# Third attention layer: a second staging buffer for the query bands, and the raw keys and value tables loaded at other steps of a head

## The reference, cut to what matters

```
rel = arange(N)[None, :] - arange(N)[:, None]
rp  = clip(rel, -31, 31) + 31                      # 63 buckets
attn = einsum('bhid,bhjd->bhij', q * scale, k)
attn = attn + take_along_axis(einsum('bhid,hdm->bhim', q * scale, rpe_k_table), rp)
attn = attn + swapaxes(take_along_axis(einsum('bhjd,hdm->bhjm', k * scale, rpe_q_table), rp), 2, 3)
attn = softmax(attn)
out  = einsum('bhij,bhjd->bhid', attn, v)
out  = out + (sums of attn over each bucket) @ rpe_v_table
x    = x + layernorm(out @ w_proj.T + b_proj)
```

## Time and profile before

| | |
|---|---|
| median of 3 runs | 2701.12 us (2699.75 to 2709.92) |
| profiled execution, device time | 2711.21 us |
| its span in the trace | 2709.3 us |
| mean granted TensorE clock | 0.83 |
| TensorE matmul / VectorE / ScalarE / GpSimd busy | 72% / 63% / 40% / 31% |
| the layer's loop in the span | from about 1573 to about 2145 us |

### The profile page before, as it was taken

The page is one execution under the profiler, slowest core; times in us unless marked ns, Lnnn a source line. Parts: engine busy times, 40 slices in busy tenths (PEclk is TensorE's granted clock), DMA queues, the critical chain, the costliest instruction groups (busy, mean ns, idle before and its releaser), DMA issues. The chain is left out here.

```text
span 2709.3 us, 46534 instructions
## 1 busy us (share of the span) xinstructions
PE 1963.8 (72%) x16472; PEld 1355.8 (50%) x16472; DVE 1715.2 (63%) x4060; ACT 1091.3 (40%) x2021; POOL 847.5 (31%) x627
## 2 busy tenths in 40 slices
PE   4888884487788873579998367777777729995446
PEld 2555553255555552467777144444444418884334
DVE  3777776575655645679999517767676763225564
ACT  2666662354444431134444215444443303331332
POOL 2000001764444501124443333444444149301001
PEclk8999998799999986679999657877776659997667
DMA  3101111000000000100000565555555240000000
GB/s 97 37 32 36 38 36 57 17 15 15 15 15 15 15 15 4 21 1 21 19 19 10 148 153 129 142 145 149 140 144 132 73 171 17 23 0 8 0 1 18
DMA packets 126467, 145.04 MB, mean 54 GB/s; under 512 B 72472, under 2 KB 100171, under 8 KB 123490
## 3 DMA queue, kind: packets, MB, share of 16 engines
q1 hardware_dynamic: 123040, 132.95, 18.8%
q10 hardware_dynamic: 3266, 9.96, 1.0%
HBM read 94.59 MB, written 40.81 MB: 50 GB/s over the span
## 5 line engine op out<-in xcount | busy, mean ns | idle before, releaser
L407 ACT ACTIVATE l0a_pr<-l0a_sm,l0a_nm 128x512 f32<-128x512 f32 x256 | 185.2, 724 | 147.3 <-DVE l0a_nm L324 146.8
L324 DVE CUSTOM_DVE_ANT_0 l0a_sm<-l0a_ps_s,l0a_tb 128x512 f32<-128x512 f32 x256 | 171.1, 686 | 93.9 <-PE l0a_ps_s L473 90.8
L481 PE MATMUL l0a_ps_p<-top_c_ident,l0a_pr 128*128 128x128 f32 x1024 | 170.4, 290 | 54.1 <-ACT l0a_pT L415 54.1
L2532 DVE STREAM_TRANSPOSE l2a_tt<-l2a_pr 128x1024 f32<-128x1024 f32 x128 | 158.1, 1235 | 73.9 <-ACT l2a_pr L2606 73.9
L2606 ACT ACTIVATE l2a_pr<-l2a_ps_s,l2a_nm 128x512 f32<-128x512 f32 x256 | 174.3, 689 | 67.8 <-DVE l2a_nm L2525 60.4
L2636 PE MATMUL l2a_ps_l<-l2a_tabq,l2a_q 128*128 128x96 f32 x512 | 112.2, 389 | 85.9 <-ACT l2a_staged L2585 80.2
L481 PEld LDWEIGHTS l0a_ps_p<-top_c_ident,l0a_pr 128*128 128x128 f32 x1024 | 110.0, 143 | 117.1 <-ACT l0a_pr L407 64.6
L2525 DVE TENSOR_REDUCE l2a_nm<-l2a_ps_s 128x2 f32<-128x1024 f32 x128 | 156.7, 1224 | 4.4
L2636 PEld LDWEIGHTS l2a_ps_l<-l2a_tabq,l2a_q 128*128 128x128 f32 x512 | 98.3, 286 | 106.0 <-ACT l2a_staged L2585 90.5
L1508 POOL TENSOR_TENSOR l1f_h<-l1f_lm,l1f_sg 128x512 f32<-128x512 f32 x72 | 92.6, 1286 | 183.8 <-DVE l1f_lm L1577 183.8
L2702 PE MATMUL l2a_ps_o<-l2a_tt,l2a_vd 128*32 128x256 f32 (+7 forms) x1472 | 133.6, 394 | 0.0
(11 more groups left out here) (501 smaller groups left out, 5281.1 us busy)
## 6 DMA issues: line engine op xcount, KB each, us to landing
l2a_rawk<-l_k SPq DMA_DIRECT2D x16, 1024.0 KB, 22.8
l2a_qb<-l_qband SPq DMA_DIRECT2D x16, 768.0 KB
l2a_sb<-l_pband SPq DMA_DIRECT2D x32, 384.0 KB
l_qband<-l2a_staged SPq DMA_DIRECT2D x14, 768.0 KB, 19.6
l0a_tb<-l_bias SPq DMA_DIRECT2D x16, 448.0 KB
l2a_ks<-l_k SPq DMA_DIRECT2D x16, 384.0 KB
l_pband<-l2a_pr SPq DMA_DIRECT2D x32, 192.0 KB, 9.0
l_pband<-l2a_pr SPq DMA_DIRECT2D x32, 144.0 KB, 2.9
```

The source lines that it names most:

```text
L324: v.tensor_tensor_reduce(sm[j % 4][:, :], ps_s[j % 2][:, :], tb[slot][:, off:off + N][:, ::-1], -1.0, 3e38, ALU.add, ALU.min, nm[:, j % 4: ...
L407: a.activation(pr[j % 4][:, :], sm[j % 4][:, :], ACT.Exp, bias=nm[:, j % 4:j % 4 + 1], scale=-1.0).then_inc(m["p_ready"], 1)
L481: last = pe.transpose(ps_p[j % 2][:, tile(k)], pr[j % 4][:, tile(k)], ident[:, :])
L2532: v.transpose(tt[n % 2][:, u * NB:(u + 2) * NB, :].rearrange("p (u k) i -> p u (k i)", u=2), pr[g // 2 % PR_RING][:, 2 * (g % 2):2 * (g % ...
```

## The change

`staged` becomes two buffers, used by turns (head modulo 2), and the copy of head h waits for the store of head h-2 and not of h-1. The key bands' rounds move from steps 0 to 2 to steps 1 to 3, on TensorE, on ScalarE and in the numbering. SyncE issues `keys(h + 2)` at step 4 and not 1, and `head_values(h)` at step 5 and not 2. GpSimd makes `values(h + 1)` at step 5 and not 7, and `expand(h + 2)` at step 7 and not 5.

```diff
@@ band_order, and the same in the programs of ScalarE and TensorE
-        if 0 <= h + 1 < HEADS and i < KEY_ROUNDS:
-            order["k", h + 1, i] = len(order) + 1
+        if 0 <= h + 1 < HEADS and 1 <= i <= KEY_ROUNDS:
+            order["k", h + 1, i - 1] = len(order) + 1
@@
-        staged = s.sb("staged", [P, NB, BAND])
+        staged = [s.sb(f"staged{i}", [P, NB, BAND]) for i in range(2)]
@@ SyncE's loop
-                    if i == 1 and h + 2 < HEADS:
-                        keys(h + 2)
                     if i == 3 and 2 <= h + 1 < HEADS:
                         head_scores(h + 1)
-                    if i == 2 and 2 <= h < HEADS:
+                    if i == 4 and h + 2 < HEADS:
+                        keys(h + 2)
+                    if i == 5 and 2 <= h < HEADS:
                         head_values(h)
@@ GpSimd's loop
-                    if i == 5 and h + 2 < HEADS:
+                    if i == 5 and 2 <= h + 1 < HEADS:
+                        values(h + 1)
+                    if i == 7 and h + 2 < HEADS:
                         expand(h + 2)
-                    if i == 7 and 2 <= h + 1 < HEADS:
-                        values(h + 1)
@@ query_evac
-                    if h >= QBAND_RING and r == 0:
-                        before = 0 if h == QBAND_RING else h - 1
+                    if h >= 4 and r == 0:
+                        before = 0 if h == 4 else h - 2
                         a.wait_ge(q_stored[before % QBAND_RING], 16 * (before // QBAND_RING + 1))
```

More of the change, by code:

```diff
@@ L2372, in q_store @@
                     else:
-                        sp.dma_start(qband[h % QBAND_RING][:, 0:ROW], staged[:, :, :].rearrange("p a n -> p (a n)")).then_inc(q_stored[h % QBAND_RING], 16)
+                        sp.dma_start(qband[h % QBAND_RING][:, 0:ROW], staged[h % 2][:, :, :].rearrange("p a n -> p (a n)")).then_inc(q_stored[h % QBAND_RING], 16)
                 def q_load(h):
@@ L2580, in query_evac @@
                     a.wait_ge(m["l_ps"], ROUND["q", h, r])
-                    if h >= QBAND_RING and r == 0:
-                        before = 0 if h == QBAND_RING else h - 1
+                    if h >= 4 and r == 0:
+                        before = 0 if h == 4 else h - 2
                         a.wait_ge(q_stored[before % QBAND_RING], 16 * (before // QBAND_RING + 1))
-                    out = pr[h - 1][:, r, 0:4 * BAND].rearrange("p (a n) -> p a n", n=BAND) if h in (1, 2) else staged[:, 4 * r:4 * r + 4, :]
+                    out = pr[h - 1][:, r, 0:4 * BAND].rearrange("p (a n) -> p a n", n=BAND) if h in (1, 2) else staged[h % 2][:, 4 * r:4 * r + 4, :]
                     a.copy(out, ps_l[:, 0:4 * BAND].rearrange("p (a n) -> p a n", n=BAND)).then_inc(m["l_ready"], 1)
@@ L2616, in _ @@
                     h, i = t // PAIRS, t % PAIRS
-                    if 0 <= h + 1 < HEADS and i < KEY_ROUNDS:
-                        key_evac(h + 1, i)
+                    if 0 <= h + 1 < HEADS and 1 <= i <= KEY_ROUNDS:
+                        key_evac(h + 1, i - 1)
                     if h + 3 < HEADS and i >= 4:
@@ L2734, in _ @@
                         scores(t)
-                    if 0 <= h + 1 < HEADS and i < KEY_ROUNDS:
-                        key_bands(h + 1, i)
+                    if 0 <= h + 1 < HEADS and 1 <= i <= KEY_ROUNDS:
+                        key_bands(h + 1, i - 1)
                     if h + 3 < HEADS and i >= 4:
```

## The result

The kernel after takes 2633.58 us (median of 4 runs, 2631.59 to 2637.26) against 2704.26 us before on the same chip (4 runs): ratio 0.9741, 95% interval 0.9722 to 0.9760, so some 70 us or 2.6% faster. Forecast were 2657 us and 44 us, with a range of 2603 to 2697. The profiled execution has a span of 2630.6 us; that of before has 2709.3, and its device time lay 7 us above the median of its kernel, so the two profiles differ by 8 us more than the medians.

What follows compares the result with a forecast made beforehand. Four DMA engines carrying the skewed loads were taken to bound a head at 31 us, not 34.4. Heads 1 to 12 gain 41 us, head 13 2, head 0 2, less 1: 44 us, so 2657 us, range 2603 to 2697.

Steps and rivals of the forecast that it cites:

- Four engines set the head: Skewed loads with four batches outermost run on four DMA engines, whose queue sets what traffic a head can carry.
- 23 + 7.8 = 31 us a head: Four engines' load: 23 from head 14, 5.2 raw keys, 2.1 store, 0.5 for `kshift` and table; 34.4 us now.
- The 23 us from head 14: Four engines' working time in head 14, which loads no raw keys and stores no query bands: some 23 us.
- Second buffer: ScalarE's wait for `staged`'s store, 9.5 us a head, goes in heads 1 to 12; gain 3.4 us each, 41 in all.
- rival B: The wait only changes its name, as head 13's 33.0 us suggest: gain 17 us or less, 2684 to 2700; chance 0.19.
- Raw keys at step 4: Keys leave the burst at the head's start and land at +28, `xk` ready at +32.8; the move costs nothing.
- a head of at least 29.2 us: Condition of the later keys: `xk` ready at +32.8, wanted by TensorE 3.6 us into the next head.
- Key bands a step later: TensorE and ScalarE work moved from step 0 to 3: taken as 0 us a head; 2 us gained in head 0.
- Compute floor of 25.8 us: Shortest head the compute engines allow, read from heads 14 and 15, which take 25.8 us each.
- Rival A: Keys out of the burst slow nothing, heads fall toward 25.8 us: 2589 us, halfway 2625; range 2589 to 2635, chance 0.23.
- Rival C: Raw keys land later than 33.5 us into a head, TensorE stands in step 1: 65 us slower, 2766 us; chance 0.10.
- SyncE itself is held as well: SyncE's queue in the burst before the change: two issues starting at 1806.21 said to take 5.20 us together.

Runs made afterwards that it cites:

- e4: Kernel after, with each skewed load (query bands, band of the exponentials) issued as four DMAs of one batch each; ratio 0.9465 to the kernel before, median 2558.9 us.
- e5: Kernel before, with both skewed loads split into four DMAs of one batch each, nothing else changed; ratio 0.9485 to the kernel before, median 2564.2 us.
- e7: Kernel after, plus a second, unread 1024 KB load behind each load of raw keys from head 2 on; ratio 0.9931 to the kernel before.
- e8: Kernel after, plus an unread 768 KB store behind each store of the staging buffer from head 3 on; ratio 0.9821 to the kernel before.
- e1: Kernel before with the second staging buffer alone, every load at its old step; ratio 1.0023 to the kernel before, median 2709.9 us.
- e2: Whole change without the second staging buffer: all moves, one buffer; ratio 0.9722 to the kernel before, median 2627.8 us.
- e9: All moves with one staging buffer, but the key bands left at steps 0 to 2; ratio 0.9886 to the kernel before.

## Why the prediction was right, and where it was not

*Four engines set the head: right.* It was read from the DMA share and is shown by e4 and e5; e7 and e8 show that added traffic lengthens a head. The rule of the Trainium skill that the prediction names (DMA: Bandwidth & Descriptors, "Why a DMA increments its semaphore by 16 and not by 1") gives 16 engines where 32 rows are outermost on both sides, and 4 where one side has four batches outermost. The measured heads, 24.2 us with the split and 34.1 without it, agree.

*"23 + 7.8 = 31 us a head": the term that was mis-sized.* For keys and store I had 5.2 + 2.1 = 7.3 us, from their landings in an empty queue less 2 us each. They cost 3.7 + 1.7 = 5.4. With that the sum is 23 + 5.4 + 0.5 = 28.9, and 28.4 was measured. I took the landings in an empty queue, less a guess, for the load on the four engines. The difference between 31 and 28.4, 2.6 us in each of 12 heads, is 31 us; by the medians the gain was 27 us larger than forecast. The new sum fits the head after, not the head before: it would leave 34.4 - 28.9 = 5.5 us of idle time there, where stretches with a share under 0.20 make up 3.0 us, near my 3.4. So the sum also lacks something: I let the same bytes take the same time before and after, and they took 19.8 us of a DMA engine's time in a head before and 17.8 after. By the packets in the two traces, heads 1 to 8, both the rows of the query bands (6144 bytes; 334 ns in the mean before, 251 after) and packets of 8192 bytes, mostly raw keys (649 and 563), took less. The 23 us from head 14 were not tested by themselves.

*Second buffer: a wait of 9.5 us less in each of heads 1 to 12, of which 3.4 us are gained: wrong.* Alone it gives nothing (e1), and taken out of the change it takes nothing with it (e2). What rival B said of the wait, that it only changes its name, is true of the buffer, and the forecast's gain stood in the wrong line of the sum. That the time came out within the range owes something to luck: the whole gain was put down to a part that gives none, and the parts priced at nothing gave it all.

*Raw keys at step 4: "the move costs nothing".* It gains, and I had put that gain down to the buffer. The count of the landing was good: +28 forecast, +28.5 measured, `xk` at +32.8 and +33.0. The condition drawn from it, a head of at least 29.2 us, was not. The head takes 28.4. I held the key bands of step 1 to 3.6 us after T0, but they can start later: in head 7 TensorE is there at +1.4, stands for 4.04 us and starts at +5.4. Such a wait is not free, as 35 us more of it go with the 44 us between e9 and e2; what the 46 us that are left cost is not shown.

*Key bands a step later: "between -0.5 and +0.5 us a head; I take 0": right alone, wrong in company.* With the other moves it is worth 44 / 12 = 3.7 us a head (e9). I had priced its instructions here; the step of lead that it gives back stood only in the condition under the raw keys, and in no term of the sum.

*Compute floor of 25.8 us: too high.* It was read from heads 14 and 15. Full heads take 24.0 us with the split loads (e4), but heads 14 and 15, which do less, still take 26.7 and 25.4 there, from start to start:

```profile
1942.78 0.38 SPq L2395 DMA_DIRECT2D l_pband<-l2a_pr  x1
...
1969.46 0.38 SPq L2395 DMA_DIRECT2D l_pband<-l2a_pr  x1
...
1994.86 0.38 SPq L2395 DMA_DIRECT2D l_pband<-l2a_pr  x1
```

So the last two heads are no picture of a full one, and it was not the skewed loads that made them long. Their granted clock is 0.70 in e4 where that of heads 1 to 8 is 0.96; whether that is the reason stays open.

*Rival A, the keys out of the burst.* The outcome, 2633.58 us and 28.4 us a head, lies in the part given to A (25.8 to 29.5 us, 2589 to 2635; chance 0.23) and not in the forecast's own (29.5 to 32.5 us, 2635 to 2680; 0.48), at the edge by the time. A's value of 28.5 us for a head (2625) was nearer than my 2657. Its reason, that keys beside the query bands lengthen them, fits the query bands' landing at +13.1 and not +17.2 and the shorter time of the transfers in all; its end, the compute floor, was not reached by the change.

*Rival C, keys too late: no.* They land 28.5 us after T0, before the 33.5 at which by my count a head would have become longer than before.

*"SyncE itself is held as well: the two issues that start at 1806.21 take 5.20 us together": misread.* The 5.20 us are from the start of the first to the end of the second. Each of these issues takes 0.38 us, and the second starts 4.8 us after the first. Other issues of the kernel before are long, as the last section shows.

## What to carry to other kernels

When many waits for landings stand in a profile, look at the DMA share over a few microseconds before adding a buffer. Here long stretches near 0.25 were four engines at work with a queue behind them, and a second buffer only gave the wait another name. The cure was the address pattern (a batch to a DMA, rows outermost), 5% from a few lines. And a moved load must be priced with the step at which its consumer asks for it: the moved loads without the shift of the key bands were worth 31 us, the shift without them 3, and both together 75. A head that lacks part of the work is a poor measure of a floor, as heads 14 and 15 were.

## What the runs showed of the hardware that was not expected

Each quarter of the 768 KB load landed 3.9 us after its issue in the median, 9.1 at most (e4), where GpSimd got the undivided load 17.2 us after it in the earlier trace rows and 13.1 us after it in the kernel after.

Single issues of SyncE were long while the skewed loads ran on four engines. The issue of L2347, a load of the scores' operands, took 4.5 us in the median and 10.3 at most in the loop of the kernel before, and 1.7 and 7.1 in the kernel after; with the loads split (e4) it took 0.42 in the median and 1.98 at most. The longest of before and of e4:

```profile
1656.72 10.31 SPq L2347 DMA_DIRECT2D l2a_qs<-l_q  x1
```

```profile
1760.67 1.98 SPq L2347 DMA_DIRECT2D l2a_qs<-l_q  x1
```

The same bytes took 19.8 us of a DMA engine's time in a head before and 17.8 after, when only the steps at which they are issued had changed and a buffer had been added.
